# Five affine passes per tile moved from VectorE to ScalarE, and weight loads that wait for less, in an 8-core BitLinear / gated-recurrence kernel

## The chip, the cores and the metric

The kernel runs on the eight cores of one Trainium2 chip. Each core takes two of the sixteen sequences and works alone; nothing passes between cores. The time is that of the slowest core, in microseconds (us) on the device. Three runs of the kernel before gave 16274.02 to 16311.62 us, median 16280.46.

## The reference

One "macaron" layer over x of shape 16 x 4096 x 1024:

```
x = x + 0.5 * ffn(layernorm(x))
x = x + recurrence(layernorm(x))          # h = a*h + b along the sequence
x = x + 0.5 * ffn(layernorm(x))

ffn(x):  h = gelu(bitlinear(x, w1, b1));  return bitlinear(h, w2, b2)      # 1024 -> 4096 -> 1024
bitlinear(x, w, b):
    xn = x * rsqrt(mean(x*x) + 1e-5)                    # per token
    s  = 127 / max|xn|;  xq = clip(round(xn * s)) / s   # 8-bit activations
    t  = 1 / mean|w|;    wq = clip(round(w * t), -1, 1) / t   # ternary weights
    return xq @ wq.T + b
```

The rounding is what the change touches. The kernel rounds in three steps: an affine step z = x * scale + offset (the offset is 256 for the hidden values, and 256 less the scaled mean for the inputs), a cast of z to a 16-bit integer q, and two VectorE operations that correct q against z and take the 256 off again. So each block of 1024 values per token passes through z, q, z', g.

## The kernel before, in words

The work of a core has four stages, each a block of its own. Within a block each engine has its instructions in one fixed list, in the order in which the Python code emits them; each instruction waits for counters (semaphores) of other engines and, on VectorE and ScalarE, for the instruction before it on its own engine. SP, the queue that issues all DMAs, is such a list too.

1. The weight stage (to about 1605 us). `mean_abs` reads w1 in 32 pieces of 128 x 1024 and w2 in 8 pieces of 128 x 4096 (L224): a DMA into one of two buffers `wld`, the absolute value on ScalarE into the single buffer `zw` (L227), and sums of 128 columns on VectorE (L231) with one more over those sums (L234). Every load waits for all that ScalarE and VectorE have been given so far, `w = [sch.tok("sS"), sch.tok("sV")]`. `quant_transpose` then reads the same pieces again (L275), scales on ScalarE (L279), casts (L282), makes them ternary on VectorE (L285 to L297), transposes them on TensorE (L315), copies them to `stg` (L325) and stores them to HBM through SP (L331); then the two 1024 x 1024 matrices of the recurrence, without rounding. Each scaling L279 waits for its load and for all of VectorE's work so far.
2. The first ffn stage: 64 tiles of 128 tokens. Per tile j: `stA` (input statistics, L408 to L430, then z L434, q L439, correction L442 and L445, variance), `stTr1` (transposes and their copy L505), `stB1` (first matmul L523 in eight groups of eight into two PSUM banks, VectorE's L534 takes each group out, gelu L542), `stC` (max of the 4096 hidden values L554, then four blocks `qc` of 1024: z L573, q L578, correction L581 and L584; then statistics L597 to L624) and `stB2` (per 512 values: transposes L638, their copy L646, eight matmuls L656; at the end L667, L672 and the store L676). Code order per step j: `stA(j+1)`, `stB1(j)`, `stB2(j-1)`, the load of tile j+2, `stTr1(j+1)`, `stC(j)`. `zq` and `qi` are two buffers each; block qc uses number qc % 2.
3. The recurrence stage (about 7872 to 10000 us), which the change does not touch. Its L797 is an Identity activation on ScalarE with scale and bias from columns.
4. The second ffn stage, the same code as stage 2.

Of the kernel before, what the change touches and what calls it, by code (L numbers as in the profile page):

```python
# [12 lines left out]
AF = mybir.ActivationFunctionType  # L13
ALU = mybir.AluOpType
# [76 lines left out]
def build_program(B_core=2, S_seq=4096):  # L91
# [29 lines left out]
    sch = Sched(nc, ["sC", "sW", "sLA", "sLB", "sOA", "sOB", "sO", "sT", "sV", "sS", "sG"])  # L121
    E = sch.emit
# [4 lines left out]
    with ExitStack() as top:  # L127
# [7 lines left out]
        c256 = sb("c256", [128, 1], F32)  # L135
# [14 lines left out]
        with ExitStack() as ph:  # L150
            psb = lambda name, shape, dt=F32: ph.enter_context(nc.sbuf_tensor(name, shape, dt))
            wld = [psb("p0_wld0", [128, F]), psb("p0_wld1", [128, F])]
            zw = psb("p0_zw", [128, F])
# [14 lines left out]
            with nc.Block("phase0") as blk:  # L168
# [9 lines left out]
                for vin, vdst in ((lam_in, coef_fm), (ba_in, ba_fm), (bx_in, bx_fm)):  # L178
                    E("sync", lambda q, vin=vin: q.dma_start(
                        vec8[:], vin.rearrange("(c p) -> c p", p=128)),  # L180
                      waits=[sch.tok("sT")], inc=("sC", 16))
                    E("tensor", lambda t: t.transpose(ps_bc[:, 0:8], vec8[:],
                                                      ident_f[0:8, 0:8]),
                      waits=[sch.tok("sC"), sch.tok("sV")], inc=("sT", 1))
# [31 lines left out]

                def mean_abs(w_ap, nrows, ncols, acc_base, out_sw, out_m, deq):
                    nch = nrows // 128
                    nsb = ncols // 128
                    for ci in range(nch):  # L220
                        wld_t = wld[ci % 2][:, 0:ncols]
                        sl_ = "sLA" if ci % 2 == 0 else "sLB"
                        w = [sch.tok("sS"), sch.tok("sV")]
                        E("sync", lambda q, ci=ci, wld_t=wld_t, w_ap=w_ap: q.dma_start(  # L224
                            wld_t, w_ap[ci * 128:(ci + 1) * 128, :]), waits=w, inc=(sl_, 16))
                        tq = sch.tok(sl_)
                        E("scalar", lambda s, wld_t=wld_t: s.activation(  # L227
                            zw[:, 0:ncols], wld_t, AF.Abs), waits=[tq], inc=("sS", 1))
                        tz = sch.tok("sS")
                        for sb in range(nsb):  # L230
                            E("vector", lambda v, sb=sb: v.reduce_sum(  # L231
                                acc8[:, sb:sb + 1], zw[:, sb * 128:(sb + 1) * 128],
                                axis=AX.X), waits=[tz] if sb == 0 else [], inc=("sV", 1))
                        E("vector", lambda v, ci=ci: v.reduce_sum(  # L234
                            acc32[:, acc_base + ci:acc_base + ci + 1], acc8[:, 0:nsb],
                            axis=AX.X), inc=("sV", 1))
# [31 lines left out]
                def quant_transpose(w_ap, nrows, ncols, swcol, out_T, do_quant, pctr=[0]):  # L268
                    nch = nrows // 128
                    npc = ncols // 128  # L270
                    for ci in range(nch):
                        wld_t = wld[ci % 2][:, 0:ncols]
                        sl_ = "sLA" if ci % 2 == 0 else "sLB"
                        w = [sch.tok("sT"), sch.tok("sS"), sch.tok("sV")]
# [3 lines left out]
                        if do_quant:  # L278
                            E("scalar", lambda s, wld_t=wld_t, swcol=swcol: s.activation(  # L279
                                zw[:, 0:ncols], wld_t, AF.Identity, scale=swcol),  # L280
                              waits=[tq, sch.tok("sV")], inc=("sS", 1))
                            E("scalar", lambda s: s.copy(qw[:, 0:ncols], zw[:, 0:ncols]),  # L282
# [19 lines left out]
                        else:  # L302
                            E("vector", lambda v, wld_t=wld_t: v.tensor_copy(
                                twbf[:, 0:ncols], wld_t),
                              waits=[tq, sch.tok("sT")], inc=("sV", 1))
                            src = twbf
# [36 lines left out]
        def ffn_phase(name, src_ap, dst_ap, src_tok_fn, store_toks_out, entry):  # L343
            NT = NTOK // 128
            with ExitStack() as ph:
# [23 lines left out]
                with nc.Block(name) as blk:  # L369
# [28 lines left out]
                    def stA(j):  # L398
                        if j >= NT:
# [34 lines left out]
                        E("vector", lambda v: v.tensor_scalar(  # L434
                            zq[0][:], xt, col(18), col(19), op0=ALU.mult, op1=ALU.add),
                          waits=[tcols, t2.get("zq0free"),
                                 tiles.get(j - 1, {}).get("r1")], inc=("sV", 1))
                        tz1 = sch.tok("sV")
                        E("scalar", lambda s: s.copy(qi[0][:], zq[0][:]), waits=[tz1],  # L439
                          inc=("sS", 1))  # L440
# [108 lines left out]
                    def stC(j):  # L549
# [14 lines left out]
                        for qc in range(4):  # L564
# [6 lines left out]
                            else:  # L571
                                wz.append(tj["r2"][qc - 2])
                            E("vector", lambda v, qc=qc, p2=p2, col=col: v.tensor_scalar(  # L573
                                zq[p2][:], hbuf[:, qc * 1024:(qc + 1) * 1024], col(12), 256.0,
                                op0=ALU.mult, op1=ALU.add), waits=wz, inc=("sV", 1))
                            tz2 = sch.tok("sV")
                            wq_ = [tz2] + ([tnext.get("r1")] if qc == 0 else [])
# [433 lines left out]
```

How the kernel before makes its waits and increments, by code:

```python
            def body(engine, ops=ops):  # L74
                lastw = {}
                for waits, fn, inc in ops:
                    for s, v in waits:
                        if lastw.get(s, -1) >= v or v <= 0:
                            continue
                        engine.wait_ge(self.sems[s], v)
                        lastw[s] = v
                    if fn is not None:
                        ins = fn(engine)
                        if inc is not None:
                            ins.then_inc(self.sems[inc[0]], inc[1])
```

## Time and profile before

| | |
|---|---|
| median of three runs | 16280.46 us |
| the profiled execution: its time, its span | 16283.99 us, 16282.4 us |
| spans of the eight cores | 16233.5 to 16282.4 us |
| busy: TensorE, VectorE, ScalarE | 36%, 44%, 23% of the span |
| mean granted TensorE clock | 0.724 of full speed |

The page and the views are of core 5, the slowest one. PE is TensorE's matmuls, PEld its weight loads, DVE is VectorE, ACT is ScalarE, SPq the SP queue. In a timeline row the bracket says how long the engine stood idle before the instruction, and what released it. A share of busy time below one half on every engine says only that no engine is the limit by itself; which one is waited for has to be read from the chain and from the rows of one tile.

### The profile page before, as it was taken

What the parts mean: (1) busy time and instruction counts of PE and PEld (TensorE: products, weight loads), DVE (VectorE), ACT (ScalarE), POOL (GpSimd) and SP (SyncE); (2) the same over time, 40 slices, a digit from 0 to 9 for tenths busy, and PEclk for the clock granted to TensorE, in tenths of its full rate; (3) what the DMA queues carried; (4) which work ended last, traced back from release to release, by engine and by line L of the source; (5) the groups of instructions that cost most, each with busy time, mean ns of one, the idle gap of its engine ahead of it and who ended that gap; (6) DMA issues with size and microseconds to landing.
All of it is one profiled execution on the core that took longest, in us unless ns stands there. A gap on an engine that the chain in (4) does not pass through costs nothing.

```text
span 16282.4 us, 93702 instructions; the slowest of 8 cores (16233.5 to 16282.4 us)
## 1 busy us (share of the span) xinstructions
PE 5782.5 (36%) x25251; PEld 2570.6 (16%) x25251; DVE 7142.7 (44%) x12221; ACT 3744.1 (23%) x4226; POOL 0.2 (0%) x4
## 2 busy tenths in 40 slices
PE   0001333333333333333344443333333333333334
PEld 0000111111111111111121221111111111111111
DVE  2443444444444444444333334444444444444444
ACT  1110111111111111111455663111111111111111
POOL 0000000000000000000000000000000000000000
PEclk9999766667676666767666766666676666776667
DMA  1123000000000000000010001000000000000000
GB/s 62 57 59 105 8 13 11 11 11 11 11 11 13 11 11 11 11 11 11 30 40 33 31 31 63 11 11 11 11 11 13 11 11 11 11 11 12 12 11 9
DMA packets 168286, 341.70 MB, mean 21 GB/s; under 512 B 93882, under 2 KB 94034, under 8 KB 163667
## 3 DMA queue, kind: packets, MB, share of 16 engines
q1 hardware_dynamic: 167764, 335.72, 6.1%
q8 instruction: 208, 3.41, 0.1%
q14 instruction: 314, 2.57, 0.1%
HBM read 214.04 MB, written 121.63 MB: 21 GB/s over the span
## 4 chain that ended last, share of the span: by engine, by line
DVE 38%; PE 30%; ACT 18%; issue 8%; DMA 3%; DVEq 1%; SPq 1%; ACTq 0%
PE f_po L656 14%; PE f_pm L523 10%; DVE f_bnh L597 4%; DVE f_zq L581 4%; DVE f_g L584 4%; ACT f_gs L646 4%; DVE colp L554 3%; ACT f_qi L578 3%; DVE f_zq L573 2%; DMA p_wld<-L_ffn_w 2%; PE f_pt L638 2%; ACT f_h L542 2%; DVEq L80 1%; PE g_pg L844 1%; DVE f_xb L667 1%
## 5 line engine op out<-in xcount | busy, mean ns | idle before, releaser
L523 PE MATMUL f_pm<-f_w1T,f_r1T 128*128 128x512 bf16 x8192 | 2136.7, 427 | 6476.6 <-DVE f_h L534 6277.6
L656 PE MATMUL f_po<-f_w2T,f_gs 128*128 128x512 bf16 x8192 | 2332.8, 436 | 1228.9 <-ACT f_gs L646 1228.9
L523 PEld LDWEIGHTS f_pm<-f_w1T,f_r1T 128*128 128x128 bf16 x8192 | 860.7, 107 | 7711.9 <-issue 6993.4
L667 DVE SCALAR_TENSOR_TENSOR f_xb<-f_po,colp,f_xb 128x512 f32<-128x512 f32 x256 | 192.2, 751 | 3708.8 <-PE f_pt L495 3588.4
L534 DVE SCALAR_TENSOR_TENSOR f_h<-f_pm,colp,b1c 128x512 f32<-128x512 f32 x1024 | 769.2, 751 | 1144.7 <-PE f_pm L523 970.7
L646 ACT COPY f_gs<-f_pt 128x512 bf16<-128x512 bf16 x1024 | 600.1, 586 | 2570.1 <-PE f_pt L638 2551.6
L656 PEld LDWEIGHTS f_po<-f_w2T,f_gs 128*128 128x128 bf16 x8192 | 803.5, 106 | 2348.4 <-issue 1786.0
L578 ACT CAST f_qi<-f_zq 128x1024 int16<-128x1024 f32 x512 | 534.7, 1044 | 2387.9 <-DVE f_zq L573 2387.9
L581 DVE SCALAR_TENSOR_TENSOR f_zq<-f_zq,f_qi 128x1024 f32<-128x1024 f32 x512 | 627.6, 1226 | 636.3 <-ACT f_qi L578 636.3
L597 DVE BATCH_NORM_STATS2 f_bnh<-f_h 128x6 f32<-128x512 f32 x1024 | 710.9, 694 | 108.2 <-DVE f_bnh L597 2.8
L584 DVE SCALAR_TENSOR_TENSOR f_g<-f_zq,f_qi 128x1024 bf16<-128x1024 f32 x512 | 627.4, 1225 | 55.7 <-DVE f_zq L581 1.8
L542 ACT ACTIVATE f_h<-f_h 128x2048 f32<-128x2048 f32 x256 | 489.0, 1910 | 476.9 <-DVE f_h L534 475.5
L554 DVE TENSOR_REDUCE colp<-f_h 128x1 f32<-128x4096 f32 x128 | 565.8, 4420 | 27.7 <-DVE f_xb L672 23.5
L844 PE MATMUL g_pg<-g_xnTb,g_waT 128*128 128x512 bf16 x1024 | 372.9, 530 | 385.3 <-ACT g_it L862 358.3
L616 ACT ACT_TABLE_LOAD x128 | 164.2, 1283 | 1380.6 <-DVE colp L613 1380.6
L638 PE MATMUL f_pt<-ident_b,f_g 128*128 128x128 bf16 x4096 | 454.0, 241 | 26.7 <-DVE f_g L584 26.7
L542 ACT ACT_TABLE_LOAD x128 | 164.2, 1283 | 1177.2 <-DVE f_h L534 1177.2
L638 PEld LDWEIGHTS f_pt<-ident_b,f_g 128*128 128x128 bf16 x4096 | 365.0, 110 | 348.2 <-issue 166.0
L573 DVE TENSOR_SCALAR f_zq<-f_h,colp 128x1024 f32<-128x1024 f32 x512 | 385.7, 753 | 56.5 <-DVE f_g L584 1.9
L439 ACT CAST f_qi<-f_zq 128x1024 int16<-128x1024 f32 x128 | 133.7, 1044 | 1073.1 <-DVE f_zq L434 1073.1
L873 DVE TENSOR_TENSOR g_pb<-g_it,g_xnTf 128x512 f32<-128x512 f32 x128 | 88.6, 692 | 642.8 <-ACT g_it L862 642.8
L315 PE MATMUL p_pst<-ident_b,p_tern 128*128 128x128 bf16 x512 | 75.0, 300 | 811.8 <-DVE p_tern L297 743.6
(145 smaller groups left out, 6012.9 us busy)
## 6 DMA issues: line engine op xcount, KB each, us to landing
p_wld<-L_ffn_w SPq DMA_DIRECT2D x64, 512.0 KB, 3.9
p_wld<-L_ffn_w SPq DMA_DIRECT2D x16, 2048.0 KB, 8.1
f_xb<-L_attn_x SPq DMA_DIRECT2D x64, 512.0 KB, 3.7
xs<-f_xb SPq DMA_DIRECT2D x64, 512.0 KB, 2.6
g_xb<-xs SPq DMA_DIRECT2D x64, 512.0 KB, 5.7
xs<-g_xb SPq DMA_DIRECT2D x64, 512.0 KB, 4.4
f_xb<-xs SPq DMA_DIRECT2D x64, 512.0 KB, 3.2
y<-f_xb SPq DMA_DIRECT2D x64, 512.0 KB, 2.6
```

The source lines that it names most:

```text
L523: E("tensor", lambda t, f=f, k=k, bank=bank, j=j: t.matmul(bank[:], r1T[:, k * 256 + (j % 2) * 128: k * 256 + (j % 2) * 128 + 128], w1T[:, ...
L534: v.scalar_tensor_tensor(hbuf[:, f * 512:(f + 1) * 512], bank[:], col(20), b1c[:, f * 512:(f + 1) * 512], op0=ALU.mult, op1=ALU.add),
L542: E("scalar", lambda s, h0=h0: s.activation(hbuf[:, h0:h0 + 2048], hbuf[:, h0:h0 + 2048], AF.Gelu), waits=[tok], inc=("sS", 1))
L554: E("vector", lambda v: v.reduce_max(col(0), hbuf[:], axis=AX.X, apply_absolute_value=True), waits=[tj["gelu"][1]], inc=("sV", 1))
L573: E("vector", lambda v, qc=qc, p2=p2, col=col: v.tensor_scalar(zq[p2][:], hbuf[:, qc * 1024:(qc + 1) * 1024], col(12), 256.0, op0=ALU.mult ...
L578: E("scalar", lambda s, p2=p2: s.copy(qi[p2][:], zq[p2][:]), waits=wq_, inc=("sS", 1))
L581: E("vector", lambda v, p2=p2: v.scalar_tensor_tensor(zq[p2][:], zq[p2][:], -0.5, qi[p2][:], op0=ALU.add, op1=ALU.is_ge), waits=[tq2], inc ...
L584: tok = E("vector", lambda v, qc=qc, p2=p2, j=j: v.scalar_tensor_tensor(gbuf[j % 2][:, qc * 1024:(qc + 1) * 1024], zq[p2][:], -256.0, qi[p ...
L597: E("vector", lambda v, i8=i8: v.bn_stats(bnh[:, i8 * 6:(i8 + 1) * 6], hbuf[:, i8 * 512:(i8 + 1) * 512]), waits=w, inc=("sV", 1))
L638: E("tensor", lambda t, fc=fc, half=half, ci=ci, j=j: t.transpose(ptr2[:, half * 2048 + ci * 512: half * 2048 + ci * 512 + 128], gbuf[j % ...
L646: tok = E("scalar", lambda s, psrc=psrc, half=half: s.copy(gstg2[half][:], psrc), waits=[ttr, st["gstg"].get(half)], inc=("sS", 1))
L656: E("tensor", lambda t, fc=fc, n=n, pi=pi, half=half: t.matmul(po[n][:], gstg2[half][:, pi * 128:(pi + 1) * 128], w2T[:, fc * D + n * 512: ...
```

## The change

```diff
--- before.py
+++ after.py
@@ -214,23 +214,28 @@
                                                               AF.Copy, scale=0.5),
                       waits=[sch.tok("sT")], inc=("sS", 1))
 
+                wfree = {}
+
                 def mean_abs(w_ap, nrows, ncols, acc_base, out_sw, out_m, deq):
                     nch = nrows // 128
                     nsb = ncols // 128
+                    zwfree = None
                     for ci in range(nch):
                         wld_t = wld[ci % 2][:, 0:ncols]
                         sl_ = "sLA" if ci % 2 == 0 else "sLB"
-                        w = [sch.tok("sS"), sch.tok("sV")]
+                        w = [wfree.get(ci % 2)]
                         E("sync", lambda q, ci=ci, wld_t=wld_t, w_ap=w_ap: q.dma_start(
                             wld_t, w_ap[ci * 128:(ci + 1) * 128, :]), waits=w, inc=(sl_, 16))
                         tq = sch.tok(sl_)
                         E("scalar", lambda s, wld_t=wld_t: s.activation(
-                            zw[:, 0:ncols], wld_t, AF.Abs), waits=[tq], inc=("sS", 1))
+                            zw[:, 0:ncols], wld_t, AF.Abs), waits=[tq, zwfree], inc=("sS", 1))
                         tz = sch.tok("sS")
+                        wfree[ci % 2] = tz
                         for sb in range(nsb):
                             E("vector", lambda v, sb=sb: v.reduce_sum(
                                 acc8[:, sb:sb + 1], zw[:, sb * 128:(sb + 1) * 128],
                                 axis=AX.X), waits=[tz] if sb == 0 else [], inc=("sV", 1))
+                        zwfree = sch.tok("sV")
                         E("vector", lambda v, ci=ci: v.reduce_sum(
                             acc32[:, acc_base + ci:acc_base + ci + 1], acc8[:, 0:nsb],
                             axis=AX.X), inc=("sV", 1))
@@ -271,7 +276,7 @@
                     for ci in range(nch):
                         wld_t = wld[ci % 2][:, 0:ncols]
                         sl_ = "sLA" if ci % 2 == 0 else "sLB"
-                        w = [sch.tok("sT"), sch.tok("sS"), sch.tok("sV")]
+                        w = [wfree.get(ci % 2)]
                         E("sync", lambda q, ci=ci, wld_t=wld_t, w_ap=w_ap: q.dma_start(
                             wld_t, w_ap[ci * 128:(ci + 1) * 128, :]), waits=w, inc=(sl_, 16))
                         tq = sch.tok(sl_)
@@ -279,6 +284,7 @@
                             E("scalar", lambda s, wld_t=wld_t, swcol=swcol: s.activation(
                                 zw[:, 0:ncols], wld_t, AF.Identity, scale=swcol),
                               waits=[tq, sch.tok("sV")], inc=("sS", 1))
+                            wfree[ci % 2] = sch.tok("sS")
                             E("scalar", lambda s: s.copy(qw[:, 0:ncols], zw[:, 0:ncols]),
                               inc=("sS", 1))
                             tqq = sch.tok("sS")
@@ -303,6 +309,7 @@
                             E("vector", lambda v, wld_t=wld_t: v.tensor_copy(
                                 twbf[:, 0:ncols], wld_t),
                               waits=[tq, sch.tok("sT")], inc=("sV", 1))
+                            wfree[ci % 2] = sch.tok("sV")
                             src = twbf
                         tsrc = sch.tok("sV")
                         for q4 in range(npc // 4):
@@ -431,13 +438,11 @@
                                                                      op=ALU.add), inc=("sV", 1))
                         tcols = sch.tok("sV")
                         tj["tcols"] = tcols
-                        E("vector", lambda v: v.tensor_scalar(
-                            zq[0][:], xt, col(18), col(19), op0=ALU.mult, op1=ALU.add),
+                        E("scalar", lambda s: s.activation(
+                            zq[0][:], xt, AF.Identity, bias=col(19), scale=col(18)),
                           waits=[tcols, t2.get("zq0free"),
-                                 tiles.get(j - 1, {}).get("r1")], inc=("sV", 1))
-                        tz1 = sch.tok("sV")
-                        E("scalar", lambda s: s.copy(qi[0][:], zq[0][:]), waits=[tz1],
-                          inc=("sS", 1))
+                                 tiles.get(j - 1, {}).get("r1")], inc=("sS", 1))
+                        E("scalar", lambda s: s.copy(qi[0][:], zq[0][:]), inc=("sS", 1))
                         tq1 = sch.tok("sS")
                         E("vector", lambda v: v.scalar_tensor_tensor(
                             zq[0][:], zq[0][:], -0.5, qi[0][:], op0=ALU.add, op1=ALU.is_ge),
@@ -570,11 +575,10 @@
                                 wz.append(t2.get("zq1free"))
                             else:
                                 wz.append(tj["r2"][qc - 2])
-                            E("vector", lambda v, qc=qc, p2=p2, col=col: v.tensor_scalar(
-                                zq[p2][:], hbuf[:, qc * 1024:(qc + 1) * 1024], col(12), 256.0,
-                                op0=ALU.mult, op1=ALU.add), waits=wz, inc=("sV", 1))
-                            tz2 = sch.tok("sV")
-                            wq_ = [tz2] + ([tnext.get("r1")] if qc == 0 else [])
+                            E("scalar", lambda s, qc=qc, p2=p2, col=col: s.activation(
+                                zq[p2][:], hbuf[:, qc * 1024:(qc + 1) * 1024], AF.Identity,
+                                bias=c256[:], scale=col(12)), waits=wz, inc=("sS", 1))
+                            wq_ = [tnext.get("r1")] if qc == 0 else []
                             E("scalar", lambda s, p2=p2: s.copy(qi[p2][:], zq[p2][:]),
                               waits=wq_, inc=("sS", 1))
                             tq2 = sch.tok("sS")
```

It has two parts. In `mean_abs` and `quant_transpose` a load into `wld[0]` or `wld[1]` now waits only for the instruction that last read that buffer (`wfree`), and the absolute value, which writes the single `zw`, waits for the sums that read it before (`zwfree`). In `stA` and `stC` the affine step z moves from VectorE (L434, L573) to ScalarE as an Identity activation with scale and bias, ahead of the cast that was there; what VectorE's step waited for is now waited for by ScalarE, and the cast follows it on the same engine.

ScalarE's list over one steady tile of the first ffn stage, from the copy of the input transposes (`f1_r1T`) to the gelu (`f1_h`); `f1_zq` and `f1_qi` are z and q, `colp` holds per-token columns. Before:

```order
L505 COPY f1_r1T<-f1_pt2 128x4x128 x2
L578 CAST f1_qi0<-f1_zq0 128x1024
L578 CAST f1_qi1<-f1_zq1 128x1024
L578 CAST f1_qi0<-f1_zq0 128x1024
L578 CAST f1_qi1<-f1_zq1 128x1024
L616 ACTIVATE colp<-colp 128x1
L439 CAST f1_qi0<-f1_zq0 128x1024
L475 ACTIVATE colp<-colp 128x1
L542 ACTIVATE f1_h<-f1_h 128x2048 x2
```

After:

```order
L510 COPY f1_r1T<-f1_pt2 128x4x128 x2
L578 ACTIVATE f1_zq0<-f1_h,c256,colp 128x1024
L582 CAST f1_qi0<-f1_zq0 128x1024
L578 ACTIVATE f1_zq1<-f1_h,c256,colp 128x1024
L582 CAST f1_qi1<-f1_zq1 128x1024
L578 ACTIVATE f1_zq0<-f1_h,c256,colp 128x1024
L582 CAST f1_qi0<-f1_zq0 128x1024
L578 ACTIVATE f1_zq1<-f1_h,c256,colp 128x1024
L582 CAST f1_qi1<-f1_zq1 128x1024
L620 ACTIVATE colp<-colp 128x1
L441 ACTIVATE f1_zq0<-f1_xb2,colp 128x1024
L445 CAST f1_qi0<-f1_zq0 128x1024
```

The five z passes of a tile stand in ScalarE's list, each directly ahead of its cast; their order among the other instructions is as before.

VectorE's list over the same blocks, from the reciprocal of the maximum to the statistics. Before:

```order
L560 TENSOR_SCALAR colp<-colp 128x1
L573 TENSOR_SCALAR f1_zq0<-f1_h,colp 128x1024
L581 SCALAR_TENSOR_TENSOR f1_zq0<-f1_zq0,f1_qi0 128x1024
L584 SCALAR_TENSOR_TENSOR f1_g0<-f1_zq0,f1_qi0 128x1024
L573 TENSOR_SCALAR f1_zq1<-f1_h,colp 128x1024
L581 SCALAR_TENSOR_TENSOR f1_zq1<-f1_zq1,f1_qi1 128x1024
L584 SCALAR_TENSOR_TENSOR f1_g0<-f1_zq1,f1_qi1 128x1024
```

After:

```order
L565 TENSOR_SCALAR colp<-colp 128x1
L585 SCALAR_TENSOR_TENSOR f1_zq0<-f1_zq0,f1_qi0 128x1024
L588 SCALAR_TENSOR_TENSOR f1_g0<-f1_zq0,f1_qi0 128x1024
L585 SCALAR_TENSOR_TENSOR f1_zq1<-f1_zq1,f1_qi1 128x1024
L588 SCALAR_TENSOR_TENSOR f1_g0<-f1_zq1,f1_qi1 128x1024
L585 SCALAR_TENSOR_TENSOR f1_zq0<-f1_zq0,f1_qi0 128x1024
L588 SCALAR_TENSOR_TENSOR f1_g0<-f1_zq0,f1_qi0 128x1024
```

The correction of one block now follows that of the block before directly; the z pass that stood between them is gone from this list.

SP's list at the end of `mean_abs` and the start of `quant_transpose`, with the counters that each DMA waits for (sV VectorE, sS ScalarE, sT TensorE). Before:

```order
L224 DMA p_wld<-L_ffn_w 128x1024 [waits sS,sV] x31
L224 DMA p_wld<-L_ffn_w 128x4096 [waits sS,sV] x8
L275 DMA p_wld<-L_ffn_w 128x1024 [waits sT,sS,sV]
L331 DMA wq1T<-p_stg 128x4x128 [waits sV] x2
L275 DMA p_wld<-L_ffn_w 128x1024 [waits sT,sS]
```

After:

```order
L227 DMA p_wld<-L_ffn_w 128x1024 x2
L227 DMA p_wld<-L_ffn_w 128x1024 [waits sS] x30
L227 DMA p_wld<-L_ffn_w 128x4096 [waits sS] x8
L280 DMA p_wld<-L_ffn_w 128x1024 [waits sS]
L338 DMA wq1T<-p_stg 128x4x128 [waits sV] x2
L280 DMA p_wld<-L_ffn_w 128x1024 [waits sS]
```

The loads of `mean_abs` stand one behind another and keep fewer waits; in `quant_transpose` a load still stands behind the two stores of the piece before it, and these wait for VectorE.

## Rows read from the trace of the kernel before

**Rows 1.** The page, the chain that ended last: share of the span by engine.

```profile
DVE 38%; PE 30%; ACT 18%; issue 8%; DMA 3%; DVEq 1%; SPq 1%; ACTq 0%
```

**Rows 2.** Windows: length, busy us of each engine, PE clock, DMA; three stretches of tiles.

```profile
4001.36:4052.85 51.49, 2.43 (x12) 0.88 (x9) 36.69 (x65) 6.91 (x8) 0.00 (x0) 0.57 0.06 21
4052.85:4100.21 47.36, 35.77 (x159) 15.71 (x160) 8.74 (x11) 10.96 (x13) 0.00 (x0) 0.82 0.00 1
...
2582.54:2625.71 43.17, 31.58 (x159) 14.51 (x160) 8.73 (x12) 10.96 (x13) 0.00 (x0) 0.93 0.00 0
```

**Rows 3.** Timeline, stC of one tile: start, length, instruction, idle before.

```profile
4006.42 0.15 DVE L560 TENSOR_SCALAR colp<-colp 128x1 f32<-128x1 f32 x1
4006.68 0.75 DVE L573 TENSOR_SCALAR f_zq<-f_h,colp 128x1024 f32<-128x1024 f32 x1
4007.52 1.04 ACT L578 CAST f_qi<-f_zq 128x1024 int16<-128x1024 f32 x1 [7.75 <-DVE f_zq L573]
4008.67 1.23 DVE L581 SCALAR_TENSOR_TENSOR f_zq<-f_zq,f_qi 128x1024 f32<-128x1024 f32 x1 [1.24 <-ACT f_qi L578]
```

**Rows 4.** Groups by line, VectorE, stC: busy, mean ns, idle before and releaser.

```profile
L581 DVE SCALAR_TENSOR_TENSOR f_zq<-f_zq,f_qi 128x1024 f32<-128x1024 f32 x512 | 627.6, 1226 | 636.3 <-ACT f_qi L578 636.3
L584 DVE SCALAR_TENSOR_TENSOR f_g<-f_zq,f_qi 128x1024 bf16<-128x1024 f32 x512 | 627.4, 1225 | 55.7 <-DVE f_zq L581 1.8
L573 DVE TENSOR_SCALAR f_zq<-f_h,colp 128x1024 f32<-128x1024 f32 x512 | 385.7, 753 | 56.5 <-DVE f_g L584 1.9 <-DVE colp L560 0.3
```

**Rows 5.** Groups by line, ScalarE: table loads ahead of gelu; an Identity activation, recurrence stage.

```profile
L542 ACT ACT_TABLE_LOAD x128 | 164.2, 1283 | 1177.2 <-DVE f_h L534 1177.2
...
L797 ACT ACTIVATE g_xn<-g_xb,colp 128x1024 f32<-128x1024 f32 x64 | 79.3, 1239 | 43.3 <-DVE colp L793 43.3
```

**Rows 6.** Timeline, weight stage: a cast that follows an activation on ScalarE.

```profile
523.16 1.15 ACT L279 ACTIVATE p_zw<-p_wld,sw1b 128x1024 f32<-128x1024 f32 x1 [3.78 <-DMA p_wld<-L_ffn_w]
524.39 1.04 ACT L282 CAST p_qw<-p_zw 128x1024 int32<-128x1024 f32 x1
```

**Rows 7.** Timeline, stA of one tile: the column before z, the correction behind q.

```profile
4042.42 0.15 DVE L430 TENSOR_SCALAR colp<-colp 128x1 f32<-128x1 f32 x1
...
4044.73 1.23 DVE L442 SCALAR_TENSOR_TENSOR f_zq<-f_zq,f_qi 128x1024 f32<-128x1024 f32 x1 [1.24 <-ACT f_qi L439]
```

**Rows 8.** Timeline, mean_abs of w1: the first piece, the sums before the last, the last.

```profile
49.27 1.06 ACT L227 ACTIVATE p_zw<-p_wld 128x1024 f32<-128x1024 f32 x1 [3.86 <-DMA p_wld<-L_ffn_w]
...
301.90 3.01 DVE L231 TENSOR_REDUCE p_acc<-p_zw 128x1 f32<-128x128 f32 x8 [5.01 <-ACT p_zw L227]
...
309.12 1.06 ACT L227 ACTIVATE p_zw<-p_wld 128x1024 f32<-128x1024 f32 x1 [7.32 <-DMA p_wld<-L_ffn_w]
```

**Rows 9.** Timeline, mean_abs of w2: the first and the last piece.

```profile
325.96 3.62 ACT L227 ACTIVATE p_zw<-p_wld 128x4096 f32<-128x4096 f32 x1 [8.86 <-DMA p_wld<-L_ffn_w]
...
499.13 3.62 ACT L227 ACTIVATE p_zw<-p_wld 128x4096 f32<-128x4096 f32 x1 [20.94 <-DMA p_wld<-L_ffn_w]
502.85 12.36 DVE L231 TENSOR_REDUCE p_acc<-p_zw 128x1 f32<-128x128 f32 x32 [11.84 <-ACT p_zw L227]
```

**Rows 10.** Timeline, quant_transpose: two stores, the load behind them, its use.

```profile
533.72 0.42 DVE L325 COPY p_stg<-p_pst 128x512 bf16<-128x512 bf16 x1 [0.83 <-PE p_pst L315]
534.75 0.39 SPq L275 DMA_DIRECT2D p_wld<-L_ffn_w  x1
538.98 1.15 ACT L279 ACTIVATE p_zw<-p_wld,sw1b 128x1024 f32<-128x1024 f32 x1 [13.54 <-DMA p_wld<-L_ffn_w]
```

**Rows 11.** The page, DMA issues: KB each and median us to landing.

```profile
p_wld<-L_ffn_w SPq DMA_DIRECT2D x64, 512.0 KB, 3.9
p_wld<-L_ffn_w SPq DMA_DIRECT2D x16, 2048.0 KB, 8.1
```

**Rows 12.** Timeline, the maximum L554 of the first and the last tile, first ffn stage.

```profile
1649.85 4.42 DVE L554 TENSOR_REDUCE colp<-f_h 128x1 f32<-128x4096 f32 x1 [2.11 <-ACT f_h L542]
...
7820.82 4.42 DVE L554 TENSOR_REDUCE colp<-f_h 128x1 f32<-128x4096 f32 x1 [0.18 <-DVE f_xb L672]
```

## The prediction

> **What bounds the kernel now.** Read first the page's chain of the work that ended last: VectorE holds 38% of the span, TensorE 30%, ScalarE 18% [rows 1]. No engine is busy half the time, so the reader should look for engines that wait for each other. The windows over one tile show it: from the maximum L554 to the first L534 VectorE works 36.69 us of 51.49 and TensorE 2.43; then, until the next L554, TensorE works 35.77 us of 47.36 and VectorE 8.74 [rows 2]. The two halves take turns. TensorE has done two of its eight groups ahead and stands still until VectorE, through stC and stA, comes to take them out of PSUM. So what is saved on the way from L554 to the first L534 is saved once per tile, 128 times. Next the timeline of stC: z 0.75 us on VectorE, q 1.04 on ScalarE, then the correction; VectorE idles 1.24 us before each L581 [rows 3], and the means over all 512 blocks say the same [rows 4]. Last the timelines of the weight stage: ScalarE waits about 7.3 us for each piece of w1 [rows 8] and up to 21 us for one of w2 [rows 9], since the next load starts only when the sums of the last piece are done.
>
> **stC.** One block costs, by the means, 0.753 (z) + 1.243 (idle, 636.3/512) + 1.226 + 0.109 + 1.225 + 0.110 (the idle time before L584 and L573 over 512) = 4.67 us [rows 4]; four blocks and the 0.11 ahead of the first z make 18.77 us from the end of L560. After the change VectorE's list holds only the eight corrections, and the reader must ask when the first may start and whether any later one waits. The first: 0.09 for the signal from VectorE to ScalarE (L573 ends at 4007.43, L578 starts at 4007.52) [rows 3], z as Identity with scale and bias from columns 1.24, for which the nearest row is the same shape in the recurrence stage [rows 5], 0.08 from an activation to the cast behind it [rows 6], the cast 1.04, and 0.11 back [rows 3]: 2.56 us. Then ScalarE runs ahead: block 1 has a buffer of its own and waits for nothing but the scale, so its q is ready 1.24 + 0.08 + 1.04 + 0.09 + 0.11 = 2.56 us after that of block 0, while VectorE needs 2 x 1.335 = 2.67 for the two corrections of a block. Blocks 2 and 3 wait for the correction two blocks before; that leaves z 2 at the end of block 0's corrections, again 2.56 us ahead of need against 2.67. So VectorE goes through without a gap, but with only 0.1 us to spare: 2.56 + 8 x 1.335 = 13.24 us. Saved: 5.53 us a tile. If the cover failed by a few tenths in three blocks it would cost 0.3 to 1 us a tile, which goes into the range. Between the ends "each block serial" (below, a loss) and "no first z at all" (8 x 1.335, a gain of 8.1) I take this value, since every duration in it has its own row.
>
> **stA.** Here one block stands alone, so nothing overlaps. Before, from the end of L430 to L442: 4044.73 - 4042.57 = 2.16 us [rows 7]. After: the same 2.56 as above. Cost: 0.40 us a tile. ScalarE has nothing else to do then (its list has the square root of the tile before, long done), so no queue stands behind it. Both together: 5.53 - 0.40 = 5.13, times 128 = 657 us less.
>
> A rule speaks against moving z. The row: 0.753 us for z on VectorE against 1.239 for the same shape on ScalarE [rows 4, 5], so the trace agrees that the operation itself gets slower. The Trainium skill, "ScalarE: Activation LUTs", section "Rules for kernel authors", says that adds and multiplies belong on VectorE. By that rule the five passes would cost 5 x 0.49 us more per tile; by the rows, four of five are hidden behind corrections that VectorE has to do anyway. What it would take for the rule to win is the first rival.
>
> **mean_abs.** A piece of w1 takes (309.12 - 49.27)/31 = 8.38 us [rows 8]. After, loads run up to two pieces ahead; a load lands in 3.9 us, one of w2 in 8.1 [rows 11], and has a whole piece's time to spare. What is left is absolute value, sums, and their two signals, because `zw` is one buffer: 1.06 + 0.10 (the gap that rows 9 show) + 3.01 + 0.09 = 4.26 us; the last small sum falls beside the next absolute value. 31 x 4.12 = 128 us, and the first piece, which now is loaded during the bias broadcasts, gives its 3.8 us of waiting back: 132. A piece of w2 takes (499.13 - 325.96)/7 = 24.74 us; after, 3.62 + 0.10 + 12.36 + 0.09 = 16.17; 7 x 8.57 = 60, and the 8.8 us that ScalarE waited for the first [rows 9]: 69. Bounds: if eight cores reading together doubled the landing times, w1 would still be covered (7.8 us against two pieces, 8.5) and w2 too (16.2 against 16.2), so I keep 201 us, with 170 as the low end.
>
> **quant_transpose.** Here the edit gives almost nothing. SP's list is in order, and the next load stands behind the two stores of the piece before it; the second store waits for the copy L325, which is VectorE's last work on that piece. The trace shows the load following that copy: L325 ends at 534.14, the load is issued at 534.75 and used at 538.98 [rows 10]. Taking its own wait away leaves it there. Only the very first load has no store ahead of it: 3.7 us, the idle time ahead of its first L279 [rows 6]. At most a wait less per load saves some hundredths of a microsecond, 55 times, 5 us at the most. Taken: 204 us for the whole weight stage.
>
> **TensorE's clock.** The second half of a tile is not a constant. It took 47.36 us with a mean granted clock of 0.82 in one tile and 43.17 with 0.93 in another, for the same instructions [rows 2]; the two levels are 2.4 GHz (1.0) and 1.2, and the long one has TensorE at the low level after its long stand and once more after the gap at the second gelu. The mean tile of the first ffn stage took (7820.82 - 1649.85)/63 = 97.95 us [rows 12]; with a first half of 51.49 that leaves 46.5 on average, near the long end. What decides is where in time TensorE resumes, and tiles in a row come close to the same length, so the present mix belongs to the present period. With a period 5 us shorter another mix must come. Its bounds are 43.2 and 47.4 each time, that is from 415 us less to 115 more over 127 tiles. I take the middle, 45.3: 1.2 x 127 = 150 us less, with half that distance either way as likely.
>
> **Sum**, against the profiled execution, 16284.0 us (its span is 1.6 us shorter; the median of the runs, 16280.5, is 3.5 us below): 16284 - 657 - 204 - 150 = 15273 us.
>
> **Rivals.** (1) Serial blocks, slower than before. If the z of a block did not start before the corrections of the block ahead are done, each block would go signal 0.09, z 1.239, 0.08, cast 1.044, 0.11, 1.226, 0.109, 1.225 = 5.12 us, 0.46 more than before: 512 x 0.46 + 128 x 0.40 = 287 us more, 204 less in the weight stage, the clock as it is: 16367 us. It decides as soon as stC and stA together lose more than 1.6 us a tile. Against it: block 1's z waits for a buffer that was free two tiles ago. This is the sign the skill's rule above would give. Chance 0.03. (2) Identity needs its function table reloaded behind the gelu: 1.283 us, the length of the load ahead of the gelu [rows 5], on the way to the first z, 128 times = 164 us: 15437. For it: no row here has Identity after gelu. Against it: in the weight stage Identity (L279) runs without one, straight after other functions [rows 6]. Chance 0.07. (3) The loads of quant_transpose do run ahead: 31 x 4.2 (534.75 to 538.98), 8 x 8.1 and 16 x about 4.2 us more are gone [rows 10, 11], 262 us: 15011. Against it is SP's order. Chance 0.03. (4) TensorE's mix stays as it was: 15423. For it: the stands of TensorE stay long (45 us instead of 50), so it resumes at the low level still. Chance 0.20. The forecast keeps 0.67.
>
> **How the numbers follow.** The likeliest case gives 15273; half the clock's distance each way and a few tenths of lost cover make its own range 15100 to 15400. Rivals 2 and 4 lie at 15437 and 15423, and I reach to 15460 above and 15090 below; beyond are rivals 1 and 3 and the ends of the clock. About 0.3%, 49 us, is what a measurement can tell from no change. Every case but the first rival is faster by far more: faster 0.96, the same 0.01 (the first rival with some of the clock's gain), slower 0.03.
>
> **What would show it.** In the changed profile: the correction in stC should have idle time before it only once per tile, about 2.5 us, not four times 1.24; z should read 1.24 us with no table load in its group; L554 to first evacuation should be about 46.4 us, with TensorE's half between 43 and 47.9 and a higher mean clock than 0.724 if the clock term is right; w1's pieces 4.3 us apart, w2's 16.2; the load in quant_transpose still issued right behind the second store. Wrong would be corrections that wait before every block (rival 1), corrections longer than 1.23 us while ScalarE works beside them, or a TensorE half whose mean does not fall.

## The result, and the profile after

The changed kernel takes 15135.0 us (median of 8 runs, 15119.98 to 15153.99) against 16279.44: ratio 0.9296, 95% interval 0.9286 to 0.9306. The forecast was 15273 us, range 15090 to 15460. The profiled execution took 15135.2 us; its slowest core is core 0, while before it was core 5. The lines in this section are of core 0. Where a difference of a few us matters, core 5 is compared with core 5 below: 16282.4 and 15122.2 us, 1160 less.

The chain that ended last has nearly the shares of [rows 1], over a shorter span (the page):

```profile
DVE 38%; PE 30%; ACT 19%; issue 8%; DMA 2%; DVEq 2%; SPq 1%; ACTq 0%
```

One tile's stC in the timeline of the kernel after (start, length, instruction, idle before; L578 is z, L582 q, L585 and L588 the corrections), to be read beside [rows 3]:

```profile
3015.07 0.15 DVE L565 TENSOR_SCALAR colp<-colp 128x1 f32<-128x1 f32 x1
3015.32 1.24 ACT L578 ACTIVATE f_zq<-f_h,c,colp 128x1024 f32<-128x1024 f32 x1 [6.89 <-DVE colp L565]
3016.65 1.04 ACT L582 CAST f_qi<-f_zq 128x1024 int16<-128x1024 f32 x1
3017.79 1.24 ACT L578 ACTIVATE f_zq<-f_h,c,colp 128x1024 f32<-128x1024 f32 x1
3017.80 1.23 DVE L585 SCALAR_TENSOR_TENSOR f_zq<-f_zq,f_qi 128x1024 f32<-128x1024 f32 x1 [2.58 <-ACT f_qi L582]
3019.11 1.04 ACT L582 CAST f_qi<-f_zq 128x1024 int16<-128x1024 f32 x1
3019.14 1.23 DVE L588 SCALAR_TENSOR_TENSOR f_g<-f_zq,f_qi 128x1024 bf16<-128x1024 f32 x1
3020.46 1.24 ACT L578 ACTIVATE f_zq<-f_h,c,colp 128x1024 f32<-128x1024 f32 x1 [0.30 <-DVE f_g L588]
3020.54 1.22 DVE L585 SCALAR_TENSOR_TENSOR f_zq<-f_zq,f_qi 128x1024 f32<-128x1024 f32 x1 [0.17 <-DVE f_g L588]
...
3028.64 6.27 DVE L601 BATCH_NORM_STATS2 f_bnh<-f_h 128x6 f32<-128x512 f32 x8
```

The second z runs beside the first correction. After the first block VectorE waits for nobody: ahead of the next L585 it stands idle for 0.17 us, behind its own L588. L601, the statistics, ends the way. The means by line answer to [rows 4, 5]:

```profile
L578 ACT ACTIVATE f_zq<-f_h,c,colp 128x1024 f32<-128x1024 f32 x512 | 634.9, 1240 | 984.7 <-DVE colp L565 886.6 <-DVE f_g L588 85.0 <-ACT f_qi L582 0.8
L588 DVE SCALAR_TENSOR_TENSOR f_g<-f_zq,f_qi 128x1024 bf16<-128x1024 f32 x512 | 627.2, 1225 | 55.3 <-DVE f_zq L585 1.4
L585 DVE SCALAR_TENSOR_TENSOR f_zq<-f_zq,f_qi 128x1024 f32<-128x1024 f32 x512 | 627.1, 1225 | 400.8 <-ACT f_qi L582 332.9 <-DVE f_g L588 67.8
```

A tile has two parts, which are called halves here though they are not equal: the first half, from the maximum over the hidden values (L554, after: L559) to the first take-out of a matmul group (L534, after: L539), and the TensorE half, from there to the next maximum. By windows (length, busy of each engine, PE clock), to be read beside [rows 2]: a first half, and the TensorE halves of two tiles.

```profile
3010.02:3056.59 46.57, 2.27 (x11) 0.83 (x9) 32.84 (x59) 13.11 (x13) 0.00 (x0) 0.57 0.06 23
3056.59:3101.73 45.14, 33.55 (x159) 15.13 (x160) 8.74 (x12) 10.96 (x13) 0.00 (x0) 0.88 0.00 0
3147.94:3190.69 42.75, 31.15 (x159) 14.45 (x160) 8.73 (x11) 10.96 (x13) 0.00 (x0) 0.94 0.00 1
```

The first half lost 5 us, as the work moved suggests. But the TensorE half, in which no instruction was changed, is shorter too, at a higher granted clock: 0.88 and 0.94 here, 0.82 in the long tile of [rows 2]. In the weight stage (timeline) w1's pieces now follow each other in about 4.3 us and wait for VectorE, no longer for DMA [rows 8]; in quant_transpose the second load is issued behind the copy L332 that the stores wait for, as before [rows 10]:

```profile
55.48 1.06 ACT L230 ACTIVATE p_zw<-p_wld 128x1024 f32<-128x1024 f32 x1 [3.20 <-DVE p_acc L235]
59.75 1.06 ACT L230 ACTIVATE p_zw<-p_wld 128x1024 f32<-128x1024 f32 x1 [3.21 <-DVE p_acc L235]
...
332.74 0.42 DVE L332 COPY p_stg<-p_pst 128x512 bf16<-128x512 bf16 x1 [0.83 <-PE p_pst L322]
333.70 0.46 SPq L280 DMA_DIRECT2D p_wld<-L_ffn_w  x1
337.41 1.15 ACT L284 ACTIVATE p_zw<-p_wld,sw1b 128x1024 f32<-128x1024 f32 x1 [12.96 <-DMA p_wld<-L_ffn_w]
```

### The profile page after: what moved, and what is told of

Read it like the earlier page. It is cut to its first block, busy times and chain, and to the rows that moved or that the text cites. A ratio compares the mean times of both kernels' runs of the same rounds, so it can differ in the third digit from the quotient of the medians.

```text
span 15133.7 us, 93515 instructions; the slowest of 8 cores (15092.0 to 15133.7 us)
## 1 busy us (share of the span) xinstructions
PE 5436.0 (36%) x25251; PEld 2481.1 (16%) x25251; DVE 6647.0 (44%) x11581; ACT 4537.7 (30%) x4866; POOL 0.2 (0%) x4
## 4 chain that ended last, share of the span: by engine, by line
DVE 38%; PE 30%; ACT 19%; issue 8%; DMA 2%; DVEq 2%; SPq 1%; ACTq 0%
PE f_po L660 14%; PE f_pm L528 10%; DVE f_bnh L601 5%; DVE f_g L588 4%; DVE f_zq L585 4%; ACT f_gs L650 4%; DVE colp L559 4%; PE f_pt L642 2%; ACT f_h L547 2%; DVEq L80 2%; DMA p_wld<-L_ffn_w 1%; PE g_pg L848 1%; DVE f_xb L671 1%; DVE f_h L539 1%; ACT f_zq L578 1%
## 5 line engine op out<-in xcount | busy, mean ns | idle before, releaser
L528 PE MATMUL f_pm<-f_w1T,f_r1T 128*128 128x512 bf16 x8192 | 2056.6, 415 | 5856.6 <-DVE f_h L539 5657.3
L660 PE MATMUL f_po<-f_w2T,f_gs 128*128 128x512 bf16 x8192 | 2084.1, 400 | 1217.7 <-ACT f_gs L650 1217.7
L539 DVE SCALAR_TENSOR_TENSOR f_h<-f_pm,colp,b1c 128x512 f32<-128x512 f32 x1024 | 768.8, 751 | 1067.1 <-PE f_pm L528 893.8
L660 PEld LDWEIGHTS f_po<-f_w2T,f_gs 128*128 128x128 bf16 x8192 | 752.6, 100 | 2179.0 <-issue 1505.7
L578 ACT ACTIVATE f_zq<-f_h,c,colp 128x1024 f32<-128x1024 f32 x512 | 634.9, 1240 | 984.7 <-DVE colp L565 886.6
L585 DVE SCALAR_TENSOR_TENSOR f_zq<-f_zq,f_qi 128x1024 f32<-128x1024 f32 x512 | 627.1, 1225 | 400.8 <-ACT f_qi L582 332.9
L601 DVE BATCH_NORM_STATS2 f_bnh<-f_h 128x6 f32<-128x512 f32 x1024 | 710.6, 694 | 107.8 <-DVE f_bnh L601 2.7
L588 DVE SCALAR_TENSOR_TENSOR f_g<-f_zq,f_qi 128x1024 bf16<-128x1024 f32 x512 | 627.2, 1225 | 55.3 <-DVE f_zq L585 1.4
L559 DVE TENSOR_REDUCE colp<-f_h 128x1 f32<-128x4096 f32 x128 | 565.7, 4420 | 27.4 <-DVE f_xb L676 23.1
L582 ACT CAST f_qi<-f_zq 128x1024 int16<-128x1024 f32 x512 | 534.9, 1045 | 46.1 <-ACT f_zq L578 2.2
L441 ACT ACTIVATE f_zq<-f_xb,colp 128x1024 f32<-128x1024 f32 x128 | 158.6, 1239 | 955.2 <-DVE colp L437 955.2
```

The lines of the kernel that those rows point to most:

```text
L528: E("tensor", lambda t, f=f, k=k, bank=bank, j=j: t.matmul(bank[:], r1T[:, k * 256 + (j % 2) * 128: k * 256 + (j % 2) * 128 + 128], w1T[:, ...
L539: v.scalar_tensor_tensor(hbuf[:, f * 512:(f + 1) * 512], bank[:], col(20), b1c[:, f * 512:(f + 1) * 512], op0=ALU.mult, op1=ALU.add),
L559: E("vector", lambda v: v.reduce_max(col(0), hbuf[:], axis=AX.X, apply_absolute_value=True), waits=[tj["gelu"][1]], inc=("sV", 1))
L578: E("scalar", lambda s, qc=qc, p2=p2, col=col: s.activation(zq[p2][:], hbuf[:, qc * 1024:(qc + 1) * 1024], AF.Identity, bias=c256[:], scal ...
L582: E("scalar", lambda s, p2=p2: s.copy(qi[p2][:], zq[p2][:]), waits=wq_, inc=("sS", 1))
L585: E("vector", lambda v, p2=p2: v.scalar_tensor_tensor(zq[p2][:], zq[p2][:], -0.5, qi[p2][:], op0=ALU.add, op1=ALU.is_ge), waits=[tq2], inc ...
```

## The experiments

All times are medians, of four runs each for e1 to e11. These are three groups (e1 to e4, e5 to e8, e9 to e11), each with its own runs of `before` on the same chip: 16274.5, 16294.8 and 16277.0 us. The ratios below are to these, and a difference between kernels of two groups, or to `after`, is good to some 20 us. The halves are means on core 5 over 125 intervals. One of these is the last of the first ffn stage; no next tile is started in it, so that its first half is short (34.8 us before, 29.3 after). It lowers each mean of the first half by about 0.13 us and their differences hardly at all.

| kernel | us | first half | TensorE half |
|---|---|---|---|
| before | 16279 | 51.26 | 46.82 |
| after | 15135 | 46.36 | 44.12 |
| e1, only z moved | 15315 | 46.32 | 44.08 |
| e2, only loads | 16072 | 51.22 | 46.74 |
| e3, after + 4.93 us pad | 16102 | 51.25 | 46.90 |
| e4, z of stA back | 14997 | 45.92 | 43.44 |
| e5, after + 1.33 us pad | 15593 | 47.68 | 46.45 |
| e6, after + 2.53 us pad | 15395 | 48.88 | 43.62 |
| e7, blocks serial | 16139 | 53.53 | 44.86 |
| e8, loads ahead of stores | 14881 | 46.36 | 44.16 |
| e9, idle matmuls, both places | 14745 | 46.34 | 41.06 |
| e10, idle matmuls, first place | 14934 | 46.34 | 42.58 |
| e11, e4 + e8 + e9 | 14404 | 45.93 | 40.83 |

The theory: three terms, namely the weight stage, VectorE's way through stC and stA, and TensorE's clock, which is thought to be set by when in time TensorE resumes and so by the tile's period. The experiments change the period; the moment of resuming is not varied by itself. The rival for the third: TensorE's half is shorter because the moved work leaves its neighbours better off.

**e1 and e2, each part alone.** Each kernel has one part of the change and leaves the other out.

> Only the z passes moved; the weight stage as before. Theory (three independent terms: weight stage -201 us on the same core, first half of a tile -4.90 us, TensorE half -2.70 us, the last two 127 times): both tile terms stay, since the weight stage only shifts when the tiles begin: 16280 - 622 - 340 = 15318 us, first half 46.4, TensorE half about 44.1. Rival (the earlier start of the tiles matters for the clock): the TensorE half lies elsewhere between 43 and 47.4, time 15180 to 15740 us.

> Only the loads of the weight stage wait for less; z on VectorE as before. Theory: weight stage 200 us shorter, tiles as before (first half 51.3, TensorE half 46.8): 16280 - 200 = 16080 us. Rival (the TensorE half fell because the tiles start at another time): TensorE half 44.1 here too, 16080 - 340 = 15740 us.

Measured 15315.3 and 16072.5 us, ratios 0.9410 (0.9396 to 0.9424) and 0.9876 (0.9861 to 0.9890). The parts add up: against `before` on the same chip they gain 959 and 202, together 1161, and the whole change gained 1144 in its own runs. The loads leave the TensorE half alone (46.74).

**e3, the period put back.** A pad here is VectorE work whose result nobody reads. In stC, ahead of the sums of the statistics:

```diff
+E("vector", lambda v: v.reduce_max(col(17), hbuf[:, 0:4096], axis=AX.X), inc=("sV", 1))
+E("vector", lambda v: v.reduce_max(col(17), hbuf[:, 0:128], axis=AX.X), inc=("sV", 1))
```

> The changed kernel with 4.93 us of idle VectorE work per tile in stC (two maxima over the hidden values, 4096 and 128 columns, into an unused column), which brings the first half of a tile back to 51.3 us. Theory (the TensorE half is a matter of the period): TensorE half back near 46.8, 15135 + 128 x 4.93 + 126 x 2.7 = 16106 us. Rival (the half is shorter because the moved work itself leaves TensorE, VectorE or ScalarE better off): it stays at 44.1, 15135 + 631 = 15766 us.

Measured 16102.3 us, ratio 0.9891 (0.9875 to 0.9908). All the moved work stays on ScalarE, only the period is that of before, and the TensorE half is back at 46.90. The rival falls. The windows show it over 63 tiles of the first ffn stage, core 5 (before, after, e3; the first number after the stretch is its length, the one before the last two the clock, averaged over both halves):

```profile
1649.85:7820.82 6170.97, 2362.46 (x10576) 1031.83 (x10576) 2850.14 (x4695) 1124.83 (x1321) 0.00 (x0) 0.70 0.03 11
```

```profile
1449.36:7141.33 5691.97, 2192.21 (x10576) 986.45 (x10576) 2610.08 (x4381) 1513.63 (x1635) 0.00 (x0) 0.73 0.03 12
```

```profile
1444.01:7626.93 6182.92, 2379.93 (x10576) 1034.95 (x10576) 2904.17 (x4508) 1515.06 (x1635) 0.00 (x0) 0.69 0.03 11
```

The same 10576 matmuls keep TensorE busy for 2362, 2192 and 2380 us.

**e5 and e6, smaller pads.** One maximum over 1024 columns; two, over 1024 and 896.

> The changed kernel with 1.33 us of idle VectorE work per tile in stC (one maximum over 1024 columns into an unused column). Rival (the TensorE half keeps its length): 15135 + 128 x 1.33 = 15305 us. Theory (the half follows where TensorE resumes, so the period): first half 47.7 us; following tile after tile the lengths that the half took in the traces so far at the same place gives a mean near 46.5 instead of 44.1: 15305 + 126 x 2.4 = 15607 us, so the pad costs almost three times its own length.

> The changed kernel with 2.53 us of idle VectorE work per tile (two maxima, over 1024 and 896 columns). Rival (half unchanged): 15135 + 324 = 15459 us. Theory: first half 48.9 us, mean TensorE half near 45.2 by the same following of lengths: 15459 + 126 x 1.1 = 15598 us, that is no slower than with half the pad.

Measured 15593.0 and 15395.1 us, ratios 0.9570 (0.9556 to 0.9584) and 0.9450 (0.9432 to 0.9468). 1.33 us of extra work a tile cost 458 us, 2.53 us cost only 260: the larger pad is the cheaper one, by far more than the spread of their runs (15589 to 15601, and 15375 to 15431). So the half does not follow the amount of work, and a half that keeps its 44.1 falls with e5 (15305 was forecast for that). How a period leads to its half is not settled. The following of lengths met e5 (46.45 against 46.5) and missed e6 by 203 us, since the half came out at 43.6 and not 45.2; there the rival's 15459 was nearer. Windows of the same 63 tiles, e5 and e6:

```profile
1445.46:7369.02 5923.56, 2339.34 (x10576) 1026.57 (x10576) 2686.92 (x4444) 1513.64 (x1635) 0.00 (x0) 0.71 0.03 11
```

```profile
1445.39:7267.62 5822.23, 2163.68 (x10576) 976.66 (x10576) 2755.40 (x4508) 1513.70 (x1635) 0.00 (x0) 0.73 0.03 11
```

**e4, the z of stA back on VectorE.** Shortened:

```diff
-E("scalar", lambda s: s.activation(zq[0][:], xt, AF.Identity, bias=col(19), scale=col(18)), ...
-E("scalar", lambda s: s.copy(qi[0][:], zq[0][:]), inc=("sS", 1))
+E("vector", lambda v: v.tensor_scalar(zq[0][:], xt, col(18), col(19), op0=ALU.mult, op1=ALU.add), ...
+E("scalar", lambda s: s.copy(qi[0][:], zq[0][:]), waits=[tz1], inc=("sS", 1))
```

> The changed kernel with the z of stA back on VectorE; the four z of stC stay on ScalarE. By the rows stA then is 0.40 us a tile shorter: 15135 - 51 = 15084 us if the TensorE half keeps its mean. Theory (period): the half may move too, by up to 1 us either way, 14960 to 15210 us, with first half 45.95. Rival (single operation is all that counts, the moved z of stA is free): 15135 us, first half 46.36.

Measured 14997.4 us, ratio 0.9213 (0.9199 to 0.9227), 138 less than after: 0.44 x 128 = 56 from the first half, 0.68 x 126 = 86 from the clock. For this lone z, which nothing overlaps, the rule weighed in the prediction holds (the Trainium skill, "ScalarE: Activation LUTs", "Rules for kernel authors": multiplies and adds on VectorE). The trace agrees with it here, by these 0.44 us. For the four z of stC it does not: with only those on ScalarE the first half is 51.26 - 45.92 = 5.34 us shorter than before the change.

**e7, no running ahead.**

```diff
+if qc > 0:
+    wz.append(tj["r2"][qc - 1])
```

> The changed kernel in which the z of each block of stC also waits for the corrections of the block before: ScalarE can no longer run ahead. Both theories: 5.12 us a block, first half 53.4 us instead of 46.4, 7.0 x 128 = 896 us more. Theory (gain in stC is the running ahead, TensorE half by period): half near 44.4: 16073 us. With the half of before (46.8): 16370 us. Rival (the gain comes from VectorE's shorter list, not from running ahead): 15135 + little, under 15400 us.

Measured 16138.6 us, ratio 0.9907 (0.9892 to 0.9921), 66 above the theory's 16073. The groups by line of e7 have the wait back before every block (L587 is the first correction):

```profile
L587 DVE SCALAR_TENSOR_TENSOR f_zq<-f_zq,f_qi 128x1024 f32<-128x1024 f32 x512 | 627.5, 1226 | 1320.3 <-ACT f_qi L584 1320.3
```

1320.3/512 = 2.58 us each time. So the gain in stC is the running ahead: without it the first half is 53.53 us, 2.3 more than before the change, and the rival falls. That e7 is still 156 us below `before` fits the loads and a TensorE half of 44.86: 201 + 126 x 1.96 - 127 x 2.27 = 160.

**e8, the loads of quant_transpose ahead of the stores.** The load of piece ci + 1 is emitted when piece ci is ternary, before its transposes. Shortened, `load` being the DMA of the loop as a function:

```diff
                         tsrc = sch.tok("sV")
+                        load(ci + 1)
                         for q4 in range(npc // 4):
```

> The changed kernel with the load of the next piece in quant_transpose issued on SP ahead of this piece's stores. Theory (SP's order was what kept these loads back): 31 x 4.3 + 7 x 9 + 14 x 4 = about 250 us less in the weight stage, tiles as they are: 14885 us. Rival (the loads are held by something else, the stores' traffic or the scaling that waits for VectorE): less than 60 us, over 15075 us.

Measured 14880.7 us, ratio 0.9133 (0.9118 to 0.9148), 254 less than after; on core 5 the tiles begin at 1137.9 us instead of 1397.4. In its timeline (core 3, its slowest) the next z (L293) starts 0.09 us after the last copy of the piece before (L342), with no wait for DMA:

```profile
331.99 0.42 DVE L342 COPY p_stg<-p_pst 128x512 bf16<-128x512 bf16 x1 [0.84 <-PE p_pst L332]
332.50 1.15 ACT L293 ACTIVATE p_zw<-p_wld,sw1b 128x1024 f32<-128x1024 f32 x1 [8.81 <-DVE p_stg L342]
```

SP's order was what kept these loads back, not the wait that the change took away.

**e9, e10, e11, TensorE kept busy.** Idle matmuls, whose result nobody reads, into `po[0]`, which the next real group overwrites. Shortened, the last line in words:

```diff
+for key, cnt in (("tcols", 10), ("r1", 16), ("tvab", 8)):       # stB1, before group 2
+    ... t.matmul(po[0][:], ident_b[:], w1T[...512 columns], start=True, stop=True), waits=[nx[key], st["po_ev"]]
+if q4 == 0: 12 of the same                                       # stB2, behind the first transposes (not in e10)
```

> The changed kernel with idle matmuls on TensorE (128 x 512 into the free bank po0, overwritten later): 34 per tile while it stands before group 2 (10 when the columns of stA are ready, 16 after its correction, 8 after its variance) and 12 in the gap at the second gelu. Theory (the spread of the TensorE half is the clock alone): with TensorE at the high level throughout, the half is the shortest one seen, 42.7, less the 2.2 us that its first matmuls still lose at the low level: about 40.5 us in every tile, granted clock 1.0 there; 15135 - 127 x 3.6 = 14680 us. Rival (the half is long for another reason, such as ScalarE beside it): it keeps its 44.1, or grows by the idle matmuls, 15135 us or more.

> As the kernel with idle matmuls in both places, but only the 34 before group 2; the gap at the second gelu stays empty. Theory: group 2 to 7 at the high level always; after the gap TensorE may still fall to the low level, in some tiles or all, 2 to 4 us each: between 14680 and 15100 us, half between 40.5 and 44.5.

> The z of stA back on VectorE, the loads of quant_transpose ahead of the stores, and both sets of idle matmuls. Theory (terms add): from the kernel with only stC's z moved, 14997, less 255 for the loads, less 127 x (43.4 - 40.5) = 368 for the clock: 14375 us. If the terms share a cause: over 14500 us.

Measured 14745.0, 14933.9 and 14404.3 us, ratios 0.9054 (0.9039 to 0.9070), 0.9172 (0.9158 to 0.9186) and 0.8846 (0.8833 to 0.8860). The timeline of e9 on core 5 (L534 is idle work, L541 the first matmul, L664 idle work, L681 the second matmul), and the window of this tile's TensorE half:

```profile
3072.55 4.43 PE L534 MATMUL f_po<-f_w1T,ident_b 128*128 128x512 bf16 x10 [33.41 <-DVE colp L437]
3077.74 7.24 PE L534 MATMUL f_po<-f_w1T,ident_b 128*128 128x512 bf16 x24 [0.76 <-DVE f_rb L450]
...
3084.82 10.52 PE L541 MATMUL f_pm<-f_w1T,f_r1T 128*128 128x512 bf16 x48
...
3095.40 2.75 PE L664 MATMUL f_po<-f_w1T,ident_b 128*128 128x512 bf16 x12
...
3099.07 1.24 PE L681 MATMUL f_po<-f_w2T,f_gs 128*128 128x512 bf16 x5 [0.92 <-ACT f_gs L671]
```

```profile
3083.09:3124.70 41.61, 33.50 (x180) 15.80 (x179) 8.73 (x11) 10.97 (x13) 0.00 (x0) 1.00 0.00 1
```

The first ten idle matmuls take 0.44 us each, at the low level of 1.2 GHz; the 48 real ones after them take 0.219 each, at the high one, and the granted clock is 1.00 over the whole half. More work on TensorE makes its half 3.1 us shorter (44.12 to 41.06), so the rival, another reason for the long halves, falls. The theory had asked for 40.5 and 14680 us; 65 us of that did not come. e10, without the twelve in the gap, lies between, as expected. e11 is the fastest version: its terms add to 14375, measured 29 more.

## Why the prediction was right, point by point

The mechanism of every term held, and one term, the clock, had the wrong size.

- **stC**: 13.24 us was predicted from the end of L560's counterpart to the statistics; the tile above has 13.42 (3015.22 to 3028.64). After the first block none waited for ScalarE (e7 shows the price if they do), so rival 1 falls. The corrections kept 1.225 us beside a working ScalarE. ScalarE's groups by line have no table load at L578; the 128 at the gelu and the 128 at the square root stand as before, so rival 2 falls. The one slip: the gap before a correction is 0.17 us, not 0.11, in three blocks of four. The mean idle time before L585 is 400.8/512 = 0.78 us, four times 3.13 instead of 2.89.
- **stA**: 0.40 more predicted, and e4 gains 0.44 by taking it back.
- Both: 5.13 us a tile predicted, 51.26 - 46.36 = 4.90 measured.
- **mean_abs**: 4.26 and 16.17 us a piece predicted; on core 5 the pieces are (179.63 - 46.12)/31 = 4.31 and (301.26 - 187.75)/7 = 16.22 us apart.
- **quant_transpose**: nothing but the first load, as predicted. From its first scaling to the first read of a tile core 5 took 1074.8 us before and 1075.7 after, so rival 3 falls, and e8 shows that the reason, SP's order, was the right one.
- Weight stage on core 5, to the first read of a tile (start of L408, then L415): 1597.9 to 1397.4, 200.5 against 204. Core 0, the slowest in the profile after, began its tiles 19.5 us later than core 5 in the same execution. Its loads in quant_transpose took longer from issue to landing (on average 4.4 us for a piece of w1 and 9.4 for one of w2, against 4.0 and 8.0 on core 5); why was not tried.
- **TensorE's clock**: the direction was right, the size was not. The step forecast 1.2 us a tile; measured are 46.82 - 44.12 = 2.70, over 126 tiles 340 us instead of 150. That is beyond the half distance that the step allowed either way. Most of it is the end point: 45.3, the middle between the shortest and the longest half, had no better ground than that no row told more. With the new period halves near 45.1 and 42.7 take turns: of 126 on core 5 none is above 46.5, where 98 were before, and 56 are below 44. The rest is the starting point: the 46.5 was taken from a mean tile that includes the short last interval of the stage, and the mean half before was 46.8. That a changed period brings another mix was right, as e3, e5 and e6 show, and that the length is a matter of the clock, as e9 shows. Which mix a period brings could not be told then, and e6 shows that it could not be told later either. Rival 4 (mix unchanged) falls.
- **The sum**, on core 5: 200.5 + 127 x 4.90 + 126 x 2.70 = 1163 us, measured 1160, forecast 1011. The clock gave 190 us more than forecast, the tiles 35 less and the weight stage 3.5 less. The slowest core ended 11.5 us later than core 5, which leaves the forecast 138 us too high. That it came no further off is in part luck: the smaller misses go the other way.

## What to carry to other kernels

Moving an operation to a slower engine paid here where that engine could start the next block while the other still worked on this one, which took a second buffer and a list without a wait in between; the lone block lost. Taking a wait off a DMA gained nothing where an older instruction of the same queue waited for the same work. Where TensorE stands still for long in every tile, read the length and the granted clock of its part in both kernels before trusting a difference of a few per cent: here a pad of the same kernel alone moved it between 43.62 and 46.90 us.

## What the runs showed that was not expected

Time is not monotone in work here: 2.53 us of extra work a tile is 198 us faster than 1.33 us, and 46 idle matmuls a tile save 390 us (15135 to 14745). A wait that is long fulfilled still costs VectorE about 0.07 us. L450, the second correction of stA, starts 0.173 us behind L447 in 125 of 128 tiles on core 5 of the kernel after, where it also waits for the transposes of the tile before, done some 40 us earlier. In the first tile of each of the two ffn stages, which has no such wait, it starts 0.104 us behind. The 0.17 us before a correction of stC is of the same size.
